# Two-layer preactivation convolution, NCHW 64 channels: statistics in two parts, one swapped row by copy, another order in a VectorE step

## The reference

```python
# layer 0: depthwise 3x3, then three 64x64 channel mixings
dw  = conv(gn(x), depthwise, groups=64)
att = softmax(attention) @ dw;  pw = pointwise @ att;  y = softmax(global_attention) @ pw
x   = x + y
# layer 1: binarised 3x3 convolution
xb  = sign(gn(x));  bw = sign(clip(w, -1, 1)) * mean(abs(clip(w, -1, 1)), per output channel)
x   = x + conv(xb, bw)
```

## Time and profile before

| what | value |
|---|---|
| median of 3 runs | 1866.14 us (1865.45 to 1870.02) |
| the profiled execution | 1866.56 us, of which the span 1864.8 |
| mean granted TensorE clock | 0.994 |
| TensorE busy | 1753.7 us, 94% |
| VectorE busy | 1683.8 us, 90% |
| ScalarE busy | 1078.4 us, 58% |
| GpSimd busy | 937.7 us, 50% |
| chain that ended last | PE 82%, DVE 7%, DMA 5%, SP queue 4% |

### The profile page before, as it was taken

One profiled execution on the slowest core, in us unless ns is written; L12 is line 12 of the kernel. 1 busy time (PEld: TensorE's weight loads), 2 busy tenths in 40 slices (PEclk: granted clock), 3 DMA queues, 4 the chain that ended last, 5 costly groups with the idle time before them and its releaser, 6 DMA issues.

```text
span 1864.8 us, 75082 instructions
## 1 busy us (share of the span) xinstructions
PE 1753.7 (94%) x32458; PEld 1341.4 (72%) x32458; DVE 1683.8 (90%) x2525; ACT 1078.4 (58%) x1410; POOL 937.7 (50%) x702
## 2 busy tenths in 40 slices
PE   0499999999999999999999999999999999999997
PEld 0299996856565555765658999689986999766554
DVE  6789999999989999999999999999999999978886
ACT  2166665666556665666656666566655666566664
POOL 1255554555455554555545555455545555555552
PEclk9999999999999999999999999999999999999999
DMA  9758786777777776777767777677777777645554
GB/s 304 187 132 203 201 200 177 201 195 206 181 188 197 200 200 180 199 200 202 201 174 193 206 201 201 175 202 202 202 186 183 202 202 200 156 118 124 123 120 115
DMA packets 333993, 346.86 MB, mean 186 GB/s; under 512 B 27152, under 2 KB 301904, under 8 KB 333664
## 3 DMA queue, kind: packets, MB, share of 16 engines
q1 hardware_dynamic: 324768, 332.94, 69.7%
q10 hardware_dynamic: 8448, 8.39, 1.5%
q0 software_dynamic: 448, 0.73, 0.2%
HBM read 134.95 MB, written 134.22 MB: 144 GB/s over the span
## 4 chain that ended last, share of the span: by engine, by line
PE 82%; DVE 7%; DMA 5%; SPq 4%; issue 1%; ACT 1%; POOL 0%; DVEq 0%; ACTq 0%
PE psA L577 63%; PE psB L577 13%; PE psL L642 3%; DMA xh<-xn 3%; PE psA L662 3%; DMA ring<-in_x 2%; SPq L304 2%; SPq L287 2%; DVE bnt L822 1%; DVE ring L1039 1%; ACT xn L449 1%; DVE psL L1030 1%; DVE smalls L938 1%; DVE xc L994 1%; DVE ring L1014 1%
## 5 line engine op out<-in xcount | busy, mean ns | idle before, releaser
L577 PE MATMUL psA<-xh,W0h 64*64 64x512 f16 (+1 forms) x9216 | 982.5, 377 | 29.1 <-DMA xh<-xn 22.7
L577 PE MATMUL psA<-xl,W0h 64*64 64x512 f16 x9216 | 969.4, 378 | 0.0
L361 POOL TENSOR_TENSOR xl<-xc,xn 128x1024 f16<-128x1024 f32 (+2 forms) x347 | 586.5, 1703 | 663.7 <-ACT xn L449 652.5
L577 PEld LDWEIGHTS psA<-xl,W0h 64*64 64x64 f16 x9216 | 540.5, 107 | 121.6 <-issue 3.8
L577 PE MATMUL psA<-xh,W0l 64*64 64x512 f16 (+1 forms) x4704 | 617.2, 376 | 0.0
L577 PEld LDWEIGHTS psA<-xh,W0h 64*64 64x64 f16 x9216 | 518.0, 106 | 131.0 <-DMA xh<-xn 38.0
L577 PE MATMUL psB<-pk,W 64*64 64x512 f16 (+2 forms) x4944 | 602.0, 362 | 3.3 <-POOL pk L370 2.4
L467 ACT ACTIVATE sg<-ring,smalls 128x1024 f16<-128x1024 f32 (+2 forms) x270 | 297.6, 1107 | 267.7 <-DVE ring L1014 266.4
L370 POOL TENSOR_TENSOR pk<-pk,sg 128x520 f16<-128x520 f16 (+2 forms) x320 | 341.7, 1076 | 203.2 <-ACT pk L475 203.2
L1014 DVE SCALAR_TENSOR_TENSOR ring<-psA,smalls,ring 128x1024 f32<-128x1024 f32 x256 | 328.4, 1283 | 123.5 <-PE psA L662 123.4
L577 PEld LDWEIGHTS psB<-pk,W 64*64 64x64 f16 x4944 | 323.8, 107 | 83.9 <-POOL pk L370 4.0
(11 more groups left out here) (113 smaller groups left out, 892.5 us busy)
## 6 DMA issues: line engine op xcount, KB each, us to landing
out_y<-ring SPq DMA_DIRECT2D x512, 256.0 KB, 3.6
ring<-in_x SPq DMA_DIRECT2D x448, 256.0 KB, 4.0
xh<-xn SPq DMA_DIRECT2D x494, 129.0 KB, 2.8
ring<-in_x SPq DMA_DIRECT2D x16, 512.0 KB, 16.5
ring<-in_x ACTq DMA_DIRECT2D x16, 512.0 KB, 16.1
xh<-xn SPq DMA_DIRECT2D x180, 32.2 KB, 2.4
xh<-xn SPq DMA_DIRECT2D x16, 96.8 KB, 2.2
pk<-in_w1T POOLq DMA_DIRECT2D x2, 144.0 KB, 6.2
```

The costliest lines, as they stand in the source:

```text
L361: ins = nc.gpsimd.tensor_tensor(xl[:, slot:slot + rows, 1:W + 1], xc[:, j:j + rows], xn[:, k:k + rows, 1:W + 1], ALU.subtract)
L577: mm = pe.matmul(bank[out0:out0 + C, c0:c1], weights[src0:src0 + C, :], src[src0:src0 + C, slot:slot + rows, width[0]:width[0] + width[1]] ...
```

## The change

1. *Statistics spread.* At step 23 `join_tuples` joins the 52 tuples of the first 26 chunks and writes the result back as half a tuple (count, mean, sum of squares); at step 29 `stats_parts` joins that with the last 12 tuples. The edge rows are taken at steps 10 and 31 (`edge_row`), and `border_of_group` moves to the end of step 31.
2. *Swap order.* The single rows of `xh` are no longer transferred: ScalarE copies them from `xc` to the other half of the partitions (`singles`), ahead of its copies to `xn`, so that a step has two swap transfers. On the SP queue the store comes before the load and is one step later (`store_chunk(t-5)`).
3. *VectorE's step.* `add_right` follows `add_left`, then `normalise(t+2)`, and `take_part` comes last.

```diff
@@ helpers @@
-    def swaps(ch):
-
-        return ([(G * ch.z, 0, 1)] if ch.at(0) else []) + [(G * ch.z + 1, 1, shared(ch))] + again(ch)
+    def singles(ch):
+
+        return ([(G * ch.z, 0, 1)] if ch.at(0) else []) + again(ch)
...
-    AGGR_STEP, SCALE_STEP = NC - 3, NC - 2
+    JOIN_STEP, AGGR_STEP, SCALE_STEP = NC - 9, NC - 3, NC - 2
+    JOINED = JOIN_STEP + BEFORE - NC + 1
@@ swap_high @@
+                k, lo, rows = buf(ch, 1), G * ch.z + 1, shared(ch)
                 for (i0, i1), (o0, o1) in ((LO, HI), (HI, LO)):
-                    for slot, j, rows in swaps(ch):
-                        k = buf(ch, j)
-                        sp.dma_start(xh[o0:o1, slot:slot + rows, :],
-                                     xn[i0:i1, k:k + rows, :]).then_inc(xh_in[n % 2], 16)
+                    sp.dma_start(xh[o0:o1, lo:lo + rows, :],
+                                 xn[i0:i1, k:k + rows, :]).then_inc(xh_in[n % 2], 16)
@@ SP's steps @@
                     swap_high(t + 1)
+                if t > LAG + 1:
+                    store_chunk(t - LAG - 2)
                 if RING <= t + RING - LAG - 3 < ALL:
                     load_chunk(t + RING - LAG - 3)
-                if t > LAG:
-                    store_chunk(t - LAG - 1)
@@ high_part @@
-                if n > 1 and ch.at(1):
-
-                    act.wait_ge(xh_in[0], xh_count(n - 1))
+                for (i0, i1), (o0, o1) in ((LO, HI), (HI, LO)):
+                    for slot, j, rows in singles(ch):
+                        nc.scalar.activation(xh[o0:o1, slot:slot + rows, 1:W + 1], xc[i0:i1, j:j + rows], ACT.Copy)
@@ VectorE @@
+            flat = bnt[:].rearrange("p n s -> p (n s)")
+            cut = 12 * JOINED
+            first_tuples, joined, last_tuples = flat[:, 0:cut], flat[:, cut - 3:cut], flat[:, cut - 3:12 * NC]
+
+            def join_tuples(img):
+                steps = Steps(stats_chain, STATS_STEPS, img)
+                dve.wait_ge(bn_done, (img - 1) * NC + JOINED)
+                steps.link(nc.vector.bn_aggr(aggr, first_tuples))
+                nc.vector.memset(joined[:, 0:1], float(JOINED * CE))
+                nc.vector.tensor_copy(joined[:, 1:2], aggr[:, 0:1])
+                steps.link(nc.vector.tensor_scalar(joined[:, 2:3], aggr[:, 1:2], float(JOINED * CE), None, ALU.mult))
...
-                steps.link(nc.vector.bn_aggr(aggr, bnt[:].rearrange("p n s -> p (n s)")))
+                steps.link(nc.vector.bn_aggr(aggr, last_tuples if img > 0 else flat))
...
                 if t > LAG:
                     add_left(*of(t - LAG - 1))
+                if t > LAG:
+                    add_right(*of(t - LAG - 1))
+                if scaling:
+                    scale_of_group(img + 1)
+                if t + 2 < ALL:
+                    dve.wait_ge(xl_rdy, t + 2)
+                    normalise(*of(t + 2))
                 for g in parts_at(t):
                     if g < ALL:
                         take_part(g)
-                if t > LAG:
-                    add_right(*of(t - LAG - 1))
                 if img + 1 < NB:
-                    if a == AGGR_STEP:
+                    if a == 10:
+                        edge_row(img + 1, 0)
+                    elif a == JOIN_STEP:
+                        join_tuples(img + 1)
+                    elif a == AGGR_STEP:
                         stats_parts(img + 1)
-                    elif a == SCALE_STEP:
-                        scale_of_group(img + 1)
-                if t + 2 < ALL:
-                    dve.wait_ge(xl_rdy, t + 2)
-                    normalise(*of(t + 2))
-                if a == SCALE_STEP and img + 1 < NB:
-                    border_of_group(img + 1)
+                    elif a == NC - 1:
+                        edge_row(img + 1, NC - 1).then_inc(edge_rdy, 1)
+                        dve.wait_ge(edge_rdy, img + 1)
+                        border_of_group(img + 1)
```

More of the change, by code:

```diff
@@ L102, in together @@
         return [(0, 0, G + 1)] if ch.at(0) else kept(ch) + again(ch)
-    def swaps(ch):
-        return ([(G * ch.z, 0, 1)] if ch.at(0) else []) + [(G * ch.z + 1, 1, shared(ch))] + again(ch)
+    def singles(ch):
+        return ([(G * ch.z, 0, 1)] if ch.at(0) else []) + again(ch)
     def xh_count(n):
-        return 32 * sum(len(swaps(Chunk(m))) for m in range(n % 2, n + 1, 2) if m > 0)
+        return 32 * (n // 2 if n % 2 == 0 else n // 2 + 1)
     def buf(ch, j):
@@ L234, in conv_preact @@
         border_rdy = sem("border_ready")
+        edge_rdy = sem("edge_row_ready")
         prep_done = sem("preparation_done")
@@ L314, in _ @@
                     swap_high(t + 1)
+                if t > LAG + 1:
+                    store_chunk(t - LAG - 2)
                 if RING <= t + RING - LAG - 3 < ALL:
                     load_chunk(t + RING - LAG - 3)
-                if t > LAG:
-                    store_chunk(t - LAG - 1)
-            for g in range(ALL - LAG - 1, ALL):
+            for g in range(ALL - LAG - 2, ALL):
                 store_chunk(g)
@@ L834, in take_borders, with edge_row @@
                 if img > 0:
-                    ins = nc.vector.reduce_sum(colp[:, :, i], edge_columns(at, G), AX.X)
+                    return nc.vector.reduce_sum(colp[:, :, i], edge_columns(at, G), AX.X)
+                return edge_row(img, i) or ins
+            def edge_row(img, i):
+                at, ins = place(img, i), None
                 for edge, (p0, p1), lo in ((0, LO, at), (NC - 1, HI, at + CE - W)):
@@ L922, in link @@
                     dve.wait_ge(self.sem, self.count)
[L924 removed]
+            STATS_STEPS = 12
             def take_part(g):
@@ L946, in stats_of_group @@
                 dve.wait_ge(gath_rdy, img + 1)
-                steps = Steps(stats_chain, STATS_STEPS, img, 1)
+                steps = Steps(stats_chain, STATS_STEPS, img, 3)
                 nc.vector.reduce_sum(st[:, 3:4], psL[:, 0, 4:8], AX.X)
@@ L959, in scale_of_group @@
             def scale_of_group(img):
-                steps = Steps(stats_chain, STATS_STEPS, img, 4)
+                steps = Steps(stats_chain, STATS_STEPS, img, 6)
                 dve.wait_ge(xc_rdy, img * NC)
@@ L975, in border_of_group @@
             def border_of_group(img):
-                steps = Steps(stats_chain, STATS_STEPS, img, 9)
+                steps = Steps(stats_chain, STATS_STEPS, img, 11)
                 steps.link(nc.vector.scalar_tensor_tensor(out=parts6[:, 0, :], in0=counts, scalar=mean0[:, 0:1],
@@ L1046, in _ @@
             link(ins)
+            spare_steps = Steps(stats_chain, STATS_STEPS, 0)
+            spare_steps.link(nc.vector.memset(spare[:], 0.0))
+            spare_steps.link(nc.vector.memset(spare[:], 0.0))
             stats_parts(0)
@@ L1070, in _ @@
                     add_layer0(*of(t - 1))
-                if a == SCALE_STEP and img + 1 < NB:
+                scaling = a == SCALE_STEP and img + 1 < NB
+                if scaling:
                     stats_of_group(img + 1)
```

4 lines of the change are left out of this document (2 added, 2 removed).

## The result

The changed kernel takes **1884.9 us** (1883.4 to 1887.5, 4 runs), the kernel before 1865.8 (1861.4 to 1870.0) beside it: ratio 1.0104 (95% interval 1.0077 to 1.0131), slower by 1.0%. The forecast was 2018; the time lies at the upper end of its first rival (1858 to 1885). Lines have moved: L994 is now L1012, L1007 is L1025, L1014 is L1032, L1030 L1048, L1034 L1052, L1039 L1057, L361 L362, L370 L371, L449 L450, L546 L547, L642 L643, L662 L663, L577 L578, L822 L823, L835 L836. L447 is the single-row copies, L956 to L958 the second join and what TensorE gathers.

The account below looks back on a forecast made before the run. TensorE (94% busy) was taken to bound the kernel, with VectorE (90%) left little room. To 1866.6 us came +151 for late steps, with image ends, SP and load at nothing: 2018 us, range 1856 to 2055.

Parts of the forecast that it names:

- first rival: At the tie of L1007 and L361 GpSimd loses, so steps stay at 6.78 or 7.58: 1872 us, chance 0.20.
- A VectorE without room: In a plain step VectorE needs 6.78 us where TensorE takes 6.71, since L994 pays L370's time in full.
- the two-piece step: One step in four, where L370 comes in two pieces and L994 wins the port: VectorE takes 5.83 us.
- The copies: ScalarE's two single-row copies in each third step and at image starts: 0.30 us each, putting L361 0.60 later.
- relief each fourth: In the first rival, steps of 6.78 or 7.58 are relieved each fourth, so VectorE drifts less than TensorE hides.
- GpSimd goes first again, L1007 ends at 8.78, and the next L1014 is at 8.70: In steps with VectorE late, L1007 waits for GpSimd's L361; such a step costs 2.0 us more than 6.71.
- +151: About 180 steps with statistics, each 0.84 us over 6.71, added to 1866.6 us; bounds 13 and 250.
- Image ends: At the ends of images swap waits of 18.3 us would clear, but VectorE arrives late: no change (-20 to +15).
- its end terms: First rival, seven image ends: gathering waits 0.5 us longer, L1007 holds 0.3 above the swap wait that goes; 0.8 each.
- Join and edge rows: The join puts 2.0 us on VectorE at step 23; the edge rows (0.8) move out of steps 29 and 30.
- The second rival: VectorE takes the port first at L994, so plain steps take 5.83, with 0.9 of room: 1848 us, chance 0.17.

Follow-up runs that it names:

- the tie turned: The changed kernel with a 128x1 memset (59 ns) on VectorE ahead of every L1025 (sums_high): 2072.1 us, ratio 1.1102.
- the statistics between: The changed kernel with the statistics pieces and column sums moved between add_right (L1057) and the normalisation (L1012): 1843.7 us, ratio 0.9876.
- the two variants of that kernel: The kernel with the statistics between, once with the swap part undone (1845.8 us), once with the edge rows at their old steps (1846.5 us).
- The tiny memset: A 59 ns memset ahead of each sums_high in the kernel with the statistics between (1841.9 us), or ahead of L1012 in the changed kernel (1883.7 us).

## Why the prediction was wrong in size

- **A VectorE without room: right.** The plain step, forecast 6.78, is 6.77 to 6.78 in the trace, the two-piece step, forecast 5.83, is 5.82 to 5.84. L1012 lasts 1.75 in plain steps, and the waits for L663 fell below 40. The Trainium skill (SBUF — State Buffer, Who interferes with whom) has it that issue order decides who blocks. The starts as recorded don't show that order: at 177.49 L1012 is recorded first and waits, at 180.42 L1025 is recorded second and doesn't.
- **The copies: right in kind, low in size.** 0.43 each (186.05, 0.85 for two), not 0.30. Steps 11 to 20 of the second image take 5.83, 6.51, 7.81, 6.78, 6.77, 6.63, 6.78, 6.78, 6.86 and 5.83 (7.56 was forecast for one with copies): 66.6 in ten, or 6.66, so VectorE keeps pace with TensorE's 6.71 by its two-piece steps. That a late VectorE makes up its plain steps in this way, rival 1 had too ("relief each fourth").
- **The term that failed: "GpSimd goes first again, L1007 ends at 8.78, and the next L1014 is at 8.70".** It was carried through 180 steps to +151; in the changed kernel sums_high keeps 0.68 in 96 of 98 such ties, and the term is worth nothing. By the sum GpSimd started 0.02 ahead (6.16 against 6.18), and the rows had it win even 0.03 behind and lose only at 0.12, so by them it had to win. But both rows were of L994 against L370, right behind L1039; L1007 against L361 is another pair, and at the same small distance it falls the other way. No row said that one pair's limit holds for the other, so the chance of 0.58 against 0.20 rested on none. With the tie turned, the mechanism is as forecast: sums_high 2.60, steps of 8.72 (8.70), TensorE waiting for it 113.9 us ("over 100"). Its size was set low: 0.95 us over 6.71 a step (chunks 4 to 22, images two to seven) where 0.84 was put, and an image 37 over where 7.1 was before: 2072 us and not 2018.
- **Image ends: set at no change, and not far off; the loss is in the steps with the new statistics.** By the ends of L663, images two to seven take 2.8 us more than before each (9.9 against 7.1), 6x2.8=17, the whole loss of the span. Of the 2.8, 1.3-0.7=0.6 lie at the end (chunks 30, 31 and 0), where the forecast had nothing and the first rival 0.8; 2.0 lie at the edge row of step 10 and at the join, for which neither sum had a term; the other 0.2 is spread over the rest. That the time falls into the first rival's range, made for its end terms, is in part luck. That rival's terms, by the matmuls' waits: the gathering was to wait 0.5 longer and waits (14.7-6.8)/7=1.1 longer; L1025 was to hold TensorE 0.3 more than the swap waits that go, and holds it (12.7+9.2-22.7)/7=-0.1. The rest is not named by these waits: of the 17.0, 9.0 are longer busy time of the same matmuls. Their ends are modelled, and a weight load that waits (20.7 us for L1025 [2.5 before], in the list of waits) shows there only in part; the mean granted clock fell from 0.994 to 0.992, worth some 4 us by my estimate. How the 9.0 divide between these stays open.
- **Join and edge rows** were costed by their lengths, 2.0 and 0.8, without the place where they fall due, and an edge row's copy at its old 0.15. On a late VectorE it waits for the port like L1012 (1.63 or 1.75, in eight of 14): lateness of 3.5 us at step 23 and 4.4 at 31, over the 2.8 that TensorE hides, so TensorE loses 1.4 us behind the join and 0.6 and 1.3 more than before behind the two edge rows.
- **The second rival** (VectorE with 0.9 us of room, 1848) came out as a kernel of its own, by another way: with the statistics between, L1012 doesn't win the port but comes after L371; VectorE's room is 0.80 in a plain step and the time 1843.7.

## What to carry to other kernels

Before adding up the prices of the parts of a change, find how much lateness the bounding engine hides and count what each part adds to it at each step: here three parts, of which no two cost anything, cost 1% together once their lateness passes it. Between two instructions that use a port which another engine holds for a known time, put work that doesn't need the port, rather than moving them next to each other. Where two engines reach for the port within some hundredths of a us of each other, step after step, the order is a switch (here 187 us for one memset of 59 ns a step), and the forecast is both values with their chances; a change that takes the two apart is better.

## What the runs showed of the hardware

- The order of two recorded starts within 0.03 us doesn't tell who gets the port. L1012, right behind L1057, is recorded 0.03 or 0.04 ahead of L371 in 110 steps of the changed kernel and waits in all of them (1.75 or a little more in 107, 1.61 or 1.62 in three); L1025, behind L836, is recorded up to 0.02 behind L362 in 98 and keeps 0.68 or 0.69 in 96. With the statistics between and in the two variants of that kernel, where it follows the join's last operation and is recorded 0.04 to 0.05 behind the subtraction, it loses in all eight cases. One row fits none of this: at 601.78 in the changed kernel L1025 is recorded 0.39 behind L362 and keeps 0.68, while L362 takes 3.01; the L844 recorded 0.01 ahead of L362 may have to do with it, but no run tests that. With a memset ahead of it, its start is still recorded 0.01 to 0.03 behind, and before the memset's own (189.03 and 189.05), and it loses. Why L1012 loses its tie wasn't tried.
- The tiny memset has no price where its engine waits anyway (1841.9 against 1843.7), and none in the late kernel ahead of the normalisation (1883.7 against 1884.9).
- A copy of 64x2 elements (L845) takes 0.15 us or, beside a GpSimd subtraction, 1.63 to 1.75; at 300.99 it ends 0.02 after it, not 0.55 as the 1024 wide L1012 does. So an instruction too small to be counted in a sum can cost 1.5 us more, about twice what an undisturbed normalisation takes (0.81).
